# A slot-scheduled decoder layer: two instructions of VectorE change places in every slot, and four lists of slot numbers are shifted

## What is computed

```python
x = layernorm(x + attention(x, Wq, bq, Wk, bk, Wv, bv, Wo, bo))
x = layernorm(x + wkv(w, u, k=x, v=ctx))
x = layernorm(x + x @ W.T + bias + sum_of_top2_experts(x))   # out_e = (x @ A_e.T) * coeff_e @ B_e.T
```

## Time and profile before

| | |
|---|---|
| time, median of 3 runs | 1584.64 us (1583.61 to 1586.76) |
| time of the profiled execution | 1586.74 us, of which the span of instructions is 1585.0 us |
| busy: PE, DVE, ACT, POOL | 97%, 84%, 70%, 64% of the span |
| mean granted TensorE clock | 0.990 of full |

### The profile page before, as it was taken

One profiled execution on the slowest core, in us unless ns is written; L12 is line 12 of the kernel. 1 busy time (PEld: TensorE's weight loads), 2 busy tenths in 40 slices (PEclk: granted clock), 3 DMA queues, 4 the chain that ended last, 5 costly groups with the idle time before them and its releaser, 6 DMA issues.

```text
span 1585.0 us, 32712 instructions
## 1 busy us (share of the span) xinstructions
PE 1537.0 (97%) x10500; PEld 1398.8 (88%) x10500; DVE 1326.2 (84%) x3435; ACT 1116.6 (70%) x2995; POOL 1006.5 (64%) x853
## 2 busy tenths in 40 slices
PE   8999999999999999999999999999999987989998
PEld 7899999999999999999999999999999976878786
DVE  6876688889889888888898989898989896877864
ACT  6777777877787878787878787868787865235333
POOL 2665586758675767676767667676767653544744
PEclk9999999999999999999999999999999998999999
DMA  8766344424441444244424442445144522112221
GB/s 296 244 229 224 99 151 141 132 67 151 148 143 51 152 151 140 61 154 153 141 61 152 140 155 51 129 150 171 48 127 153 180 68 83 54 68 92 63 86 54
DMA packets 81641, 202.62 MB, mean 128 GB/s; under 512 B 10432, under 2 KB 11072, under 8 KB 81472
## 3 DMA queue, kind: packets, MB, share of 16 engines
q1 hardware_dynamic: 81472, 200.53, 40.4%
HBM read 120.80 MB, written 37.75 MB: 100 GB/s over the span
## 4 chain that ended last, share of the span: by engine, by line
PE 83%; DVE 8%; issue 3%; POOL 2%; ACT 2%; DVEq 1%; DMA 1%; SPq 0%; POOLq 0%; ACTq 0%
PE bank L546 25%; PE bank L548 24%; PE bank L547 24%; PE bank L670 5%; PE bank L615 2%; PE bank L616 1%; PE bank L661 1%; PE bank L653 1%; PE bank L685 1%; DVE ED L1366 1%; DMA SW<-QB 1%; ACT Xh L768 0%; DVE PS L1325 0%; DVEq L1436 0%; DVE RC L1196 0%
## 5 line engine op out<-in xcount | busy, mean ns | idle before, releaser
L546 PE MATMUL bank<-Xh,W 128*128 128x256 f32 x1280 | 357.5, 279 | 4.4 <-DVE RC L1196 2.1
L548 PE MATMUL bank<-Xh,W 128*128 128x256 f32 x1280 | 356.1, 278 | 0.0
L547 PE MATMUL bank<-Xl,W 128*128 128x256 f32 x1280 | 355.8, 278 | 0.0
L1050 POOL TENSOR_TENSOR Ql<-RC,Qh 128x512 fp32r<-128x512 f32 x127 | 170.2, 1340 | 195.0 <-ACT Qh L768 195.0
L783 ACT ACTIVATE S<-S,NM 128x128 f32<-128x128 f32 (+1 forms) x512 | 228.2, 448 | 68.4 <-DVE NM L1181 67.4
L1038 POOL TENSOR_TENSOR SW<-SW,tables 128x512 f32<-128x512 f32 x128 | 174.6, 1364 | 124.6 <-DMA SW<-QB 124.6
L546 PEld LDWEIGHTS bank<-Xh,W 128*128 128x128 f32 x1280 | 241.5, 189 | 6.6 <-issue 2.8
L548 PEld LDWEIGHTS bank<-Xh,W 128*128 128x128 f32 x1280 | 241.2, 188 | 0.0
L547 PEld LDWEIGHTS bank<-Xl,W 128*128 128x128 f32 x1280 | 241.0, 188 | 0.0
L768 ACT ACTIVATE PTh<-bank 128x384 fp32r<-128x384 f32 x256 | 125.1, 489 | 152.6 <-PE bank L670 151.4
L768 ACT ACTIVATE S<-S,RL 128x128 f32<-128x128 f32 (+1 forms) x512 | 203.9, 448 | 35.0 <-DVE RL L1188 34.6
(11 more groups left out here) (161 smaller groups left out, 4425.3 us busy)
## 6 DMA issues: line engine op xcount, KB each, us to landing
W<-kept SPq DMA_DIRECT2D x140, 512.0 KB, 4.5
SW<-QB SPq DMA_DIRECT2D x256, 128.0 KB, 2.3
kept<-W SPq DMA_DIRECT2D x40, 512.0 KB, 5.0
XR<-XR SPq DMA_DIRECT2D x64, 128.0 KB, 2.3
RO<-in_xn SPq DMA_DIRECT2D x16, 512.0 KB, 4.0
KVT<-in_ctxt SPq DMA_DIRECT2D x16, 512.0 KB, 4.4
mixed<-RO SPq DMA_DIRECT2D x16, 512.0 KB, 3.8
XR<-in_xt SPq DMA_DIRECT2D x15, 512.0 KB, 4.2
```

The lines of the kernel that those rows point to most:

```text
L546: nc.tensor.matmul(dst, lhs[0], rhs[0], start=first, stop=False)
L547: nc.tensor.matmul(dst, lhs[0], rhs[1], start=False, stop=False)
L548: return nc.tensor.matmul(dst, lhs[1], rhs[0], start=False, stop=last)
L1050: gp.tensor_tensor(Q[1][:, :, :], RC[:, i % 2, :, :], Q[0][:, :, :], ALU.subtract).then_inc(q_lo, 1)
```

## The change

VectorE runs `probabilities(n)` ahead of `maxima(n)` in every slot. Of the first half's output weights the third to eighth are split at slots 5, 6, 6, 7, 8, 8 instead of 5, 5, 6, 6, 7, 7; K and V of the second half at 9, 10, 12, 13 instead of 7, 8, 10, 11. The stores of V go two slots later, those of Q and O three. Two feed-forward pieces are split one slot later and one a slot earlier; the first feed-forward load moves from slot 250 to 251, and four parts move one slot back: (3,1) from 266 to 267, (9,2) from 279 to 280, (12,0) from 284 to 285, (14,0) from 290 to 291. TensorE's opening matmuls are 14 instead of 18.

```diff
-SPLIT_AT = [[-6, -6, -2, -2, -6, -6, 0, 1, 2, 2, 3, 4] + [h // 2 + 4 for h in range(HEADS)],
-            [7, 8, 10, 11] + [h + 11 for h in range(HEADS)] + [h + 19 for h in range(HEADS)]]
+SPLIT_AT = [[-6, -6, -2, -2, -6, -6, 0, 1, 2, 2, 3, 4] + [4, 4, 5, 6, 6, 7, 8, 8],
+            [9, 10, 12, 13] + [h + 11 for h in range(HEADS)] + [h + 19 for h in range(HEADS)]]
 RELOAD_AT = [-10, -9, -6, -5] + [h - 6 for h in range(HEADS)] + [h + 3 for h in range(HEADS)]
-KEEP_AT = [2, 3, 4, 5] + [h + 4 for h in range(HEADS)] + [h + 9 for h in range(HEADS)]
+KEEP_AT = [2, 3, 6, 7] + [h + 7 for h in range(HEADS)] + [h + 12 for h in range(HEADS)]
...
-FFN_SPLIT_AT = [254, 254, 256, 257, 259, 260, 261, 262, 263, 264]
+FFN_SPLIT_AT = [254, 254, 256, 257, 259, 259, 261, 262, 264, 265]
...
-PARTS = [1, 1, 2, 3, 1, 1, 1, 2, 2, 0, 2, 0, 1, 1, 3, 1, 0, 2, 1, 3, 1, 1, 2, 1, 0, 1, 1, 1, 0]
-PARTS_AT = {250: [(0, 0)], 257: [(1, 1), (1, 2), (1, 0)], 262: [(2, 0), (2, 1)], 263: [(2, 2)]}
+PARTS = [1, 0, 3, 3, 1, 1, 1, 2, 2, 0, 2, 0, 1, 1, 2, 2, 0, 2, 1, 2, 2, 1, 2, 1, 0, 0, 2, 1, 0]
+PARTS_AT = {251: [(0, 0)], 257: [(1, 1), (1, 2), (1, 0)], 262: [(2, 0), (2, 1)], 263: [(2, 2)]}
...
             pe.wait_ge(consts, 1)
-            for _ in range(18):
+            for _ in range(14):
                 nc.tensor.matmul(tail_ps[:, 0:P], S[:, 0, 0:P], S[:, 0, 0:P], start=True, stop=True)
...
                 first_sums(n, 2)
+                probabilities(n)
                 maxima(n)
-                probabilities(n)
                 tail(n, 0)
                 x_low(n)
...
                     last.then_inc(acc_read, 1)
+                probabilities(n)
                 maxima(n)
-                probabilities(n)
                 tail(n, 0)
```

## The result

| | before | changed |
|---|---|---|
| median, us | 1584.12 (1583.47 to 1586.76, 4 runs) | 1594.73 (1592.36 to 1596.34, 4 runs) |
| profiled execution, us | 1586.74, span 1585.0 | 1596.34, span 1594.5 |

The ratio is 1.0058, 95% interval 1.0042 to 1.0074: slower by some 9 us (7 to 12). The prediction had 1583.0 us, and gave everything slower 0.13.

What follows compares the result with a forecast made beforehand. The prediction took TensorE, busy 97% of the span, as the bound, with gains only at the start and behind the last head. Its terms, 0 - 0.7 + 0 + 0 - 0.8 - 0.1 = -1.6 us, gave 1583.0 us; range 1579.5 to 1587.5.

Steps and rivals of the forecast that it cites:

- Part 1: Probabilities ahead of maxima in 256 slots: the pair ends when it ended, idle time hides later exponentials; 0, bounds 0 and +6 us.
- the new order slows the loop: Rival: later exponentials cost 0.4 us in each of 15 tails of the loop, giving 1589 us; chance 0.05.
- signs of being wrong: New waits in the loop, above all of scores for the maxima, or a half-clock stretch in slots 12 to 15.
- Part 2: First weights in other slots: 1.3 us gained by slot 10, 0.6 us lost in slots 12 to 14; -0.7 us at the start.
- The crossed order: Q0 split ahead of V0: VectorE waits for ScalarE's count in slots 12 and 13, +0.6 us; as jam rival 1587.4 to 1589.1, chance 0.08.
- Parts 3 and 4: Later stores, from slots 4 and 5 to 12 to 19, gain 0; four opening matmuls less gain 0.
- The rival with half clock at the opening: With fewer opening matmuls the first two projections run at half clock: +1.0 us (0.3 to 1.8), 1584.0 us; chance 0.04.
- Part 5: Moved feed-forward splits: PTh 0.3 us earlier for TensorE, router wait 0.5 us shorter; -0.8 us, bounds 0 and -1.
- kept as a rival: Half-clock stretches at 51 and 1340 us both go, 1.7 us each: 1579.6 us; chance 0.28.
- Part 6: Four parts a slot later: waits lost at 1485.85 us, regained at 1497.94 us; -0.1 us in the sum, bounds -1 and +2.

Runs made afterwards that it cites:

- e4: The changed kernel, with GpSimd's power (its tail place 0) ahead of the low part of the inputs: 1591.26 us, ratio 1.0038 to the kernel before.
- e12: The changed kernel, new order in every slot, with the first scan of QS one slot later: 1615.34 us, ratio 1.0204 to the kernel before.
- e1: The kernel before with only the new order, probabilities ahead of maxima in every slot: 1600.59 us, ratio 1.0092.
- e8: The kernel before with 14 opening matmuls for 18, nothing else: 1584.32 us, ratio 1.0004.
- e6: The kernel before with only the new slots of the feed-forward splits and of the four parts: 1582.83 us, ratio 0.9977.
- e10: The kernel before with the new order in slots 24, 25, 1 and 2 of every 32 alone: 1592.58 us, ratio 1.0040.
- e7: The kernel before with only the new slots of the first weights' splits and stores: 1584.97 us, ratio 1.0000.
- e9: The changed kernel with the old order and GpSimd's power ahead of the low part of the inputs: 1578.06 us, ratio 0.9963 to the kernel before.

## Why the prediction was wrong

**Part 1 failed, by its sentence that the pair ends when it ended.** That holds if PTh is there when the low part's turn comes. In the old order it nearly always was, because the maxima ran first: 3.7 us of waiting in 256 slots. With the low part ahead VectorE waits 78.2 us for PTh, in slot 24 for 1.05 us, in slot 25 for 0.27 us and in slot 2 for 0.56 us, while the scores are ready behind it. The number that I used as a cover, VectorE's 67.9 us of idle time for scores, was the time in which PTh was made; it was no slack. What part 1 said of ScalarE came as forecast: the exponentials start 0.56 us later against the scores (mean over heads 32 to 246; "up to 0.55"), and the query bias with them. In slots 24 and 25 the pair ends 1.1 us later against the scores than before. The term was given 0, with bounds of 0 and +6 us; it measured +14.6 us (12.4 to 16.8).

**The bound was too low since it priced one place.** I followed the delay to the cosine product; those waits went from 1.0 to 2.3 us only. What costs is that the steps behind the pair, which have to do with neither, move by 0.5 to 0.6 us against GpSimd's: 0.9 us in slot 25 and 0.3 to 0.7 in slot 2 per period. The rival "the new order slows the loop" had the sign and, at 1589 us, too little of the size, by a wait that hardly grew. Of its signs of being wrong the prediction had new waits in the loop right, but not their kind: no scores wait for the maxima there, they wait for Ql, and the transposes of the tail for the residual sum. That the meetings cause the two big slots is shown by e4 and e12, which take one meeting away each and leave the order. The third, slot 14, is read from the trace alone and not shown: the scan of PS takes 2.02 to 2.04 us beside Ql in all seven periods, and the cosine product behind it is late by 0.29 us; before, the scan took 1.64 us or less in five periods, but also 2.02 us in two, where it started earlier and slot 14 lost nothing. Slot 30 stays open: it gains 0.17 us in the three kernels where slot 25 loses 0.91 (the changed one, e1, e4), and in no other.

**Part 2 had its steps right, and its times partly by luck.** The projection that had waited until 50.19 us starts at 48.58 us (48.8 forecast), and the scores of slot 10, which are those of head 6, wait for Ql until 53.49 us (53.5 forecast). But 0.7 us of this stands at head 0 already, and e1 shows a cost that part 2 left out: with the order alone TensorE waits 3.18 us for the cosine product until 51.46 us, and head 6 comes 1.3 us later than before. The stretch at 51 us runs at full clock, where it was at 0.53, and the one at 34 us stays; by e8 the first is not shown to be the edit's doing. The prediction's reading, half clock behind idle times of 2 us and more and not of 1.5, does not hold: in the kernel before a wait of 2.05 us until 20.75 us is followed by full clock, one of 1.71 us until 34.12 us by half. In their own trace the first weights gain 2.5 us by slot 10 (1.3 forecast), 0.7 of it at head 0 already, and that trace runs at full clock from 10 to 60 us, without the stretch at 34 us; 1.1 us go again between heads 10 and 16 (0.6 forecast). The crossed order does what was said, only dearer: VectorE waits for ScalarE's count ahead of a split, 3.03 us in slot 12 and 1.27 us in slot 13, the second time with the product of head 13 queued behind it. TensorE's and VectorE's timelines of the changed kernel, then its stretches (us, PE, PEld, DVE, ACT and POOL busy, clock, DMA share, GB/s):

```profile
48.58 0.39 PE L546 MATMUL bank<-W,Xh 128*128 128x256 f32 x1 [0.58 <-DVE RC L1196]
...
53.49 0.38 PE L615 MATMUL bank<-KHL,Qh 128*128 128x256 f32 x1 [1.53 <-POOL Ql L1050]
...
68.39 1.12 DVE L1462 TENSOR_TENSOR W<-A2Z,W 128x512 fp32r<-128x512 f32 x1 [3.03 <-ACT W L768]
...
74.14 0.69 DVE L1462 TENSOR_TENSOR W<-A2Z,W 128x512 fp32r<-128x512 f32 x1 [1.27 <-ACT W L768]
```

```profile
33.30:36.80 3.50, 3.36 (x15) 3.14 (x16) 3.30 (x11) 2.42 (x8) 0.96 (x2) 0.57 0.67 155
51.00:54.50 3.50, 1.97 (x13) 1.55 (x12) 2.54 (x6) 3.31 (x11) 2.76 (x3) 1.00 0.08 19
1349.70:1354.60 4.90, 4.88 (x27) 4.16 (x28) 4.78 (x6) 2.64 (x6) 4.90 (x4) 1.00 0.00 0
```

The sum, -0.7 forecast, is 0 within 2 us by the times. Traces vary by 0.6 us at the start with nothing changed there (e6 at head 10, e10 at head 0), so no more can be said.

**Parts 3 and 4 were right, as far as the runs tell.** No wait for a store turned up (e7 has the stores only together with the splits). The first projection now waits for its weights, 0.86 us in e8, and that costs nothing: the third starts at 11.01 us, where it started at 11.10. The rival with half clock at the opening falls with e8, and in the changed kernel too the first two projections run at full clock.

**Part 5 was right in sign and too small:** -0.9 for parts 5 and 6 together against -3.6 us (1.9 to 5.5). Behind the last head the changed kernel has

```profile
1339.39 0.38 PE L739 MATMUL bank<-tables,SW 128*64 128x128 f32 x2 [3.47 <-DVE OTl L1269]
...
1349.72 0.66 PE L727 MATMUL bank<-tables,QB 128*128 128x128 f32 x4 [2.48 <-POOL QB L1151]
...
1497.49 0.41 PE L739 MATMUL bank<-tables,SW 128*64 128x128 f32 x2 [1.51 <-DVE SW L1421]
```

The wait of 3.08 us for the router's chain is 2.48 us (0.5 less forecast), and the stretch behind it, at 0.65 before, runs at full clock, which the prediction kept as a rival; it does so in e8 too, without these edits. The third gain was not seen at all: the hid transposes at 1327.30 us had waited 5.14 us and wait 3.47 now. The same two waits were shorter in the traces of e7 (4.08 us and none) and e10, which lack these edits, so a single trace can't price them; e6's interval can price the edits together, but how much of the 3.6 us is waits and how much clock stays open.

**Part 6** did the trade that it named: the wait of 1.45 us at 1497.94 us is gone, and one of 1.51 us stands at the hid transposes (1497.49 us, now some 9.5 us later in all).

## What to carry to other kernels

Before two steps that wait for different engines change places, look at what the first of them waits for now: an idle time that is small in one order can be small because the other step covers it. Where VectorE and GpSimd both work from SBUF, a shift of half a microsecond has no price of its own, but list the VectorE steps with two SBUF inputs that start within a microsecond of a GpSimd step, and ask which come on the wrong side of it and who waits for that. A table by slot of the period, from the starts of one instruction that every slot has, finds the few places that lose, where totals by engine show nothing: VectorE was busy for 1326.2 us before and 1326.8 after.

## What the runs showed of the hardware

An instruction of 128x2 elements took 0.16 us alone and up to 1.29 us (1.28 in slot 2) behind a GpSimd step of 128x512, and GpSimd's subtraction 2.25 us instead of 1.30 behind a VectorE scan of 1.23 us: the step that was issued second pays with most of the rest of the first (0.95 of 1.17 us for Ql, 1.12 of 1.26 for the shift, 1.08 of 1.23 for the scan of e12), whichever engine it is on and however small it is. In the kernel before five shifts in slot 2 had already met the product (1.24 to 1.26 us each), and TensorE waited 0.3 us behind four of them; so there was something to win in this place (e9).

TensorE's clock falls to half behind idle times of 1.7 to 3 us in some traces and stays full behind like ones in others (0.53 in the kernel before and 1.00 in e8, behind 1.98 and 1.95 us at the same place).
